# Moving the layer norms of batches 2 and 3 ahead of their batch and sending batch 1's through TensorE, in a fused attention and mixture-of-experts kernel

## The reference

```python
x = x + tanh(g_xattn[0]) * xattn(layernorm(x), ctx, ctx, wq, wk, wv, wo)
n = layernorm(x)                                  # 4 batches, 512 x 256 each
shared = sum over 2 experts of gelu(n @ up_s.T) @ down_s.T
probs  = softmax(n @ router_w.T)                  # 16 experts
gate   = probs where they are among the 4 highest of the token, else 0
routed = sum over 16 experts of (gelu(n @ up_r.T) * gate) @ down_r.T
out = x + tanh(g_ffn[0]) * (shared + routed)
```

## Time and profile before

| what | value |
|---|---|
| median of 3 runs | 535.67 us (534.5 to 536.22) |
| time of the profiled execution | 533.67 us |
| its span, first to last instruction | 531.9 us |
| around the span | 1.8 us |
| TensorE busy | 507.0 us, 95% of the span |
| VectorE, ScalarE, GpSimd busy | 67%, 58%, 52% |
| granted TensorE clock, mean | 0.997 |

### The profile page before, as it was taken

One profiled execution on the slowest core, in us unless ns is written; L12 is line 12 of the kernel. 1 busy time (PEld: TensorE's weight loads), 2 busy tenths in 40 slices (PEclk: granted clock), 3 DMA queues, 4 the chain that ended last, 5 costly groups with the idle time before them and its releaser, 6 DMA issues.

```text
span 531.9 us, 12294 instructions
## 1 busy us (share of the span) xinstructions
PE 507.0 (95%) x4386; PEld 421.4 (79%) x4386; DVE 355.7 (67%) x1150; ACT 310.4 (58%) x858; POOL 275.9 (52%) x213
## 2 busy tenths in 40 slices
PE   9888998999999999999999998899998999899996
PEld 5677787889988998888889786667776878678884
DVE  6868867658675677668866847486647665675554
ACT  3467767566757566766766956554536453644442
POOL 4899988779887978897998325430100010000000
PEclk9999999999999999999999999999999999999999
DMA  7362224011121101220221075514621372048021
GB/s 250 98 174 66 71 55 150 8 36 38 21 96 38 36 11 28 57 55 22 57 73 38 3 228 177 112 22 127 251 40 17 101 282 41 12 103 284 1 32 47
DMA packets 52075, 44.65 MB, mean 84 GB/s; under 512 B 33520, under 2 KB 35824, under 8 KB 52016
## 3 DMA queue, kind: packets, MB, share of 16 engines
q1 hardware_dynamic: 52016, 43.88, 29.3%
HBM read 30.62 MB, written 2.23 MB: 62 GB/s over the span
## 4 chain that ended last, share of the span: by engine, by line
PE 60%; POOL 11%; DVE 10%; issue 7%; SPq 6%; ACT 4%; DMA 2%; DVEq 0%; POOLq 0%; ACTq 0%
PE ring L1010 42%; SPq L354 5%; PE psO L1189 5%; PE psS L1010 4%; PE psS L1158 4%; PE psT L1170 4%; POOL arena L462 3%; POOL arena L464 2%; POOL prob L468 2%; DVE prob L819 2%; POOL wl L476 1%; DVE arena L768 1%; DMA pT<-pT 1%; POOL arena L455 1%; ACT oTh L563 1%
## 5 line engine op out<-in xcount | busy, mean ns | idle before, releaser
L1010 PE MATMUL ring<-xTh,wh 128*128 128x512 f32 x272 | 109.9, 404 | 1.8 <-DVE wl L840 1.4
L1010 PE MATMUL ring<-xTh,wl 128*128 128x512 f32 x272 | 106.8, 393 | 0.0
L1010 PE MATMUL ring<-xTl,wh 128*128 128x512 f32 x272 | 106.7, 392 | 0.0
L827 DVE TENSOR_TENSOR oTl<-prob,oTh 128x512 fp32r<-128x512 f32 x64 | 46.2, 722 | 58.7 <-ACT oTh L563 58.4
L468 POOL TENSOR_TENSOR prob<-prob,rinv 128x512 f32<-128x512 f32 x64 | 68.0, 1064 | 15.4 <-DVE rinv L921 15.4
L563 ACT ACTIVATE oTh<-prob 128x512 fp32r<-128x512 f32 x64 | 40.4, 631 | 60.9 <-DVE prob L819 36.1
L1010 PEld LDWEIGHTS ring<-xTh,wh 128*128 128x128 f32 x272 | 51.1, 188 | 14.9 <-issue 3.0
L637 ACT ACTIVATE pT<-psT 128x512 f32<-128x512 f32 x64 | 38.0, 593 | 40.3 <-PE psT L1170 40.3
L1010 PEld LDWEIGHTS ring<-xTh,wl 128*128 128x128 f32 x272 | 51.0, 188 | 11.3
L1010 PEld LDWEIGHTS ring<-xTl,wh 128*128 128x128 f32 x272 | 51.2, 188 | 10.9 <-issue 0.2
L547 ACT ACTIVATE sneg<-ring 128x512 f32<-128x512 f32 x72 | 42.5, 591 | 23.3 <-PE ring L1010 23.2
(11 more groups left out here) (123 smaller groups left out, 1230.3 us busy)
## 6 DMA issues: line engine op xcount, KB each, us to landing
arena<-gate_scratch SPq DMA_DIRECT2D x64, 256.0 KB, 6.3
raw<-in_e SPq DMA_DIRECT2D x18, 256.0 KB, 2.8
raw<-in_w SPq DMA_DIRECT2D x16, 256.0 KB, 3.8
arena<-arena SPq DMA_DIRECT2D x16, 256.0 KB, 3.1
pT<-pT SPq DMA_DIRECT2D x112, 32.0 KB, 2.0
arena<-arena SPq DMA_DIRECT2D x16, 192.0 KB, 3.5
out<-x SPq DMA_DIRECT2D x16, 128.0 KB, 6.2
x<-in_x SPq DMA_DIRECT2D x3, 512.0 KB, 3.8
```

The lines of the kernel that those rows point to most:

```text
L827: dve.tensor_tensor(lo, src, hi.bitcast(F32), ALU.subtract).then_inc(f_lo, 1)
L1010: last = pe.matmul(out, a, b, start=start and i == 0 and j == 0, stop=stop and i == n - 1 and j == 2, skip_group_check=check)
```

## The change

Three things change in the table of jobs and in the waits that guard them.

1. Norm 5 (batch 1) no longer goes through `turn`, `xhi` and `xlo`. Its statistics move from after step 3 to after step 4, its two halves of normalising from after step 4 to after steps 6 and 7, and after step 9 it takes the path of `xT`: 8 transposes on TensorE into the PSUM banks `psT` and `psO`, two copies by ScalarE, two subtractions by VectorE. The router follows after step 10 in place of 11, and `rexp`, `pick_a` and `pick_b` each one step sooner; `gT` stays after step 15.
2. Norms 6 and 7 (batches 2 and 3) are made earlier: the statistics after step -2 of the batch before (that is 5 steps sooner), the halves after steps -1 and 0, the `turn` after step 2 in place of 5. `xhi`, `xlo` and everything down to `gT` stand one step sooner.
3. Waits follow: `turn` waits for `z` of the batch before, batch 0's `back` no longer waits for `xlo` but for the end of the attention, and `r` waits for norm 5's `xTl`, since both use `psT`.

```diff
-        for b in range(B - 1):
-            for e, kind in ((3, "stat"), (4, "norm_a"), (4, "norm_b")):
+        for e, kind, n in ((4, "stat", B + 1), (6, "norm_a", B + 1), (7, "norm_b", B + 1), (9, "xT", B + 1),
+                           (10, "r", 1), (11, "rexp", 1), (12, "pick_a", 1), (13, "pick_b", 1), (15, "gT", 1)):
+            after[e].append((kind, n))
+        for b in range(1, B - 1):
+            for e, kind in ((-2, "stat"), (-1, "norm_a"), (0, "norm_b")):
                 after[b * NE + e].append((kind, B + b + 1))
-            for e, kind in ((5, "turn"), (9, "xhi"), (10, "xlo"), (11, "r"), (12, "rexp"), (13, "pick_a"),
-                            (14, "pick_b"), (15, "gT")):
+            for e, kind in ((2, "turn"), (8, "xhi"), (9, "xlo"), (10, "r"), (11, "rexp"), (12, "pick_a"),
+                            (13, "pick_b"), (14, "gT")):
                 after[b * NE + e].append((kind, b + 1))
...
                 elif kind == "turn":
-                    sp.wait_ge(xn_turned, n)
+                    sp.wait_ge(xn_turned, n - 1)
...
-                    act.wait_ge(xn_moved, 256 * n)
-                    if n == 1:
-                        act.wait_ge(down_pe, KC * NS)
-                    else:
-                        act.wait_ge(up_pe, NE * (n - 1))
-                        act.wait_ge(r_pe, n - 1)
+                    act.wait_ge(xn_moved, 256 * (n - 1))
+                    act.wait_ge(up_pe, NE * (n - 1))
+                    act.wait_ge(r_pe, n - 1)
...
-                act.wait_ge(xT_pe, min(j, B + 1))
-                if j > B + 1:
-                    act.wait_ge(xn_turned, j - B - 1)
+                act.wait_ge(xT_pe, min(j, B + 2))
+                if j > B + 2:
+                    act.wait_ge(xn_turned, j - B - 2)
...
-                    if n == 1:
-                        dve.wait_ge(oT_pe, CHUNKS // 2)
-                    else:
-                        dve.wait_ge(z_out, 4 * (n - 1))
+                    dve.wait_ge(z_out, 4 * (n - 1))
...
                     dve.wait_ge(y_out, GROUPS * (n + 1))
-                    if n + 1 < B:
+                    if n == 0:
+                        dve.wait_ge(oT_pe, CHUNKS // 2)
+                    elif n + 1 < B:
                         dve.wait_ge(xT_lo, B + n + 2)
...
+                elif job[0] == "xT" and job[1]:
+                    pe.wait_ge(p_out, CHUNKS)
+                    pe.wait_ge(oT_lo, CHUNKS // 2)
                 elif job[0] == "r":
-                    pe.wait_ge(p_out, CHUNKS)
+                    pe.wait_ge(xT_lo, B + 2)
                     pe.wait_ge(r_sub, job[1])
```

## The result

The changed kernel takes 523.1 us (median of 5 runs, 522.66 to 523.18) against 535.67 us (median of 5, 534.0 to 536.22): a ratio of 0.9774, 95% interval 0.9755 to 0.9793. The direction, the place and the mechanism were right; two sizes were not: what a stall costs, and how far the profile of the kernel before stood from its median. A later set of runs gave 522.84 against 535.31, ratio 0.9765 (0.9751 to 0.9778).

What follows compares the result with a forecast made beforehand. TensorE, busy 507.0 of 531.9 us, was taken as the bound, with 10.3 us of waits in the expert part. 5.4 + 4.3 = 9.7 us off gave 524.0 by the profile, 526.0 by the median; range 523.8 to 529.

Steps and rivals of the forecast that it cites:

- Part 2, the moves: Norms 6 and 7: moves done before `xhi`, all stalls of batches 1 and 2 go; 4.5 us, 4.3 counted.
- It sums to 10.3 us: TensorE's waits in the expert part, as listed: 7.2 + 2.2 + 0.9, nearly all on `rest_gated`.
- Part 1, norm 5: Batch 0: 5.49 us of stalls and 1.3 of low clock, less 0.9 for transposes; 5.4 us taken.
- it goes if the stall goes: Batch 0, after the 2.31 us stall: the low clock cost 1.3 us and vanishes with that stall.
- may stay: Batch 0's last stall, 0.47 us, may remain: table loads and `pick_a` share steps with weight rounding; 0.5 left for residues.
- L618 waits for nothing: Sign of being right: ScalarE's normalising no longer waits for GpSimd's `shift`; that wait was 3.14 us in batch 0.
- the rival named by the Trainium skill's rule: TensorE's clock falls once after the new transposes, which don't count as busy like matmuls: 1.3 us, 527.3; 5%.
- The shown median of 535.67 stands 2.0 above it, so by the median 526.0: From profiled run to median: 533.67 less 9.7 is 524.0, plus the same 2.0 gives 526.0.
- Late moves: Batches 1 and 2: moves still late, half of the two large stalls stays, perhaps a clock drop: 529; 9%.
- Router path: Batch 0 keeps its stalls, as ScalarE waits for transposes instead of moves: 528, or 529 with low clock; 9%.
- Gates held up: Small moves delay the gates' DMAs in batches 1 and 2, so every `gated` waits: 536 or more; 3%.
- No effect: VectorE's and ScalarE's work alone bounds the steps, so stalls only move: 535; 3%.

Runs made afterwards that it cites:

- part 2's: The kernel before with norms 6 and 7 made early and norm 5 left as before: 529.3 us, ratio 0.989.

## Why the prediction was right in kind and too small in size

**What bounds it, and where.** Right. All that was won lies at the places named in the earlier trace rows, and batch 3 is unchanged (0.96 and 0.97 us lost).

**Part 2, the moves.** Right in mechanism: `xhi` waits for no DMA, batches 1 and 2 lose nothing, and the traffic of the gates delayed nothing that counts: the 16 issues took 11.4 and 12.1 us beside it, not 10.5, and `xhi` still found its blocks there. The term "4.5 us; I keep 0.2 for small ones" was mis-sized: 4.3 forecast, 2.74 + 3.18 = 5.9 measured. The step that failed is the sum over the waits' view, "It sums to 10.3 us". A printed stall leaves out some 0.27 us at its two edges, and the router's 0.16 us at one. Four stalls and two waits of the router in batches 1 and 2 make 1.4 us, and the 0.2 kept for small ones was not needed; that is the difference of 1.6. The numbers to see it were there: the matmul durations of 0.50 in the earlier trace rows beside the usual 0.40.

**Part 1, norm 5.** 5.4 us forecast, 5.86 - 0.79 = 5.1 measured, but by errors that cancelled. The transposes cost 0.79 (0.9 forecast) and the router did not wait, as worked out. The stalls of 0.36 and 1.46 went. The edges of three fewer stalls gave 0.7 us more. Against that, 1.5 us of printed stalls stayed where 0.5 was allowed for. The 1.3 us of low clock are in the 8.57 and did go, but the step "it goes if the stall goes" counted as a cost of its own what was worth 0.2: without the low clock the router would have waited 0.7 us longer and the next stall been 0.3 longer, and the batch would have lost 8.36. That the sum came within 0.3 us was luck. The reason given for the stalls that "may stay", table loads and `pick_a` beside the weight rounding, was wrong: with the weight rest on VectorE they all go (two losses of 0.2 us, too short to be printed, are left), and table loads and rounding are still there. The sign "L618 waits for nothing" held for norm 5 alone; norms 6 and 7, whose `stat` and `norm_a` still stand one step apart, waited 2.3 and 1.7 us, at no cost to TensorE.

**The clock.** It did stay at 1.00 with the transposes in place, so the rival named by the Trainium skill's rule ("TensorE: Matmul & The Clock Gate", part 4) did not come about here. Two stretches of the changed kernel, the first with the eight transposes of step 9 (335.40) in it:

```profile
330.00:336.00 6.00, 6.00 (x30) 4.89 (x30) 4.09 (x6) 5.01 (x10) 3.35 (x3) 1.00 0.27 85
336.00:342.00 6.00, 6.00 (x30) 4.59 (x28) 4.39 (x8) 3.40 (x7) 2.62 (x2) 1.00 0.31 84
```

**From the profile to the median.** The second step that failed, and the larger error. "The shown median of 535.67 stands 2.0 above it, so by the median 526.0" carried the 2.0 us over to the changed kernel, as if it were a constant of the chip. It belonged to the kernel before: a longer stall in batch 2 and more low clock than in the one profiled run (1.0 to 1.6 us in three other profiles), and a later start of the expert part, by 0.3 to 0.9 us. The changed kernel has no such stall, and its profiled run (523.18) and its median (523.1) agree. Its start came at 307.10 and 306.71 in its two profiles; why its runs hold together within 0.55 us all the same isn't shown. Of the 2.9 us by which the gain was larger than forecast, 1.3 lie in the expert part (11.0 where 9.7 were summed) and 1.6 in this step. The account of the 12.6 us: 11.0 in the expert part, less 0.5 for the later start in this one profile, plus 2.0 by which the median of before stood above its profile, plus 0.1.

**The rivals.** Late moves: no. Router path: in part, 1.5 us of stalls, by a cause that wasn't named. (Its price was also added up wrongly: the stalls named, 1.36, and half of 2.31, less 0.5, do make 2.0 us, but "1.2 + 0.9 less the 0.5" makes 1.6.) Gates held up: no `gated` waits for a DMA. No effect: no.

## What to carry to other kernels

Price a stall of a matmul stream from start to start, not by the idle time that the view prints: here 0.27 us more for each, and losses of up to 0.3 us that aren't printed at all. If the kernel's runs spread more than the profile's waits explain, ask whether the spread comes from the stalls themselves, and take a second profile of the kernel before; a change that removes them can remove the distance between the profile and the median too. And before more work is moved off a busy engine, look at what its instructions last beside their undisturbed length: four subtractions given back to VectorE made it faster.

## What was not expected of the hardware

- The clock of TensorE fell behind six of nine gaps of 2.3 to 2.7 us, counted over six profiles of kernels with the old path in batch 0, and not behind the other three (2.29 us in part 2's, with a clock of 1.00 right after; 2.31 and 2.49 us in two others). It fell behind none of the gaps of 1.7 to 2.2 us. The low stretches held 7 to 13 matmuls.
- A low clock can cost next to nothing: 8.57 and 8.35 us lost in batch 0 with it, 8.36 and 8.39 without, because the next waits ended at the same time.
- One DMA issue of 16 alike can take 0.96 to 1.60 us where the others take 0.61, at the same place in the queue in all four profiles of before, and TensorE's stall behind it grows by the same amount.
- VectorE's 128x512 instructions of 0.68 us took 1.78, and its 128x1024 one 2.32 instead of 1.22, where GpSimd had begun a subtraction 0.1 to 0.6 us before; both lose 1.1 us. Where less of GpSimd's subtraction was left (begun 0.9 to 1.3 us before), the 128x512 ones took 0.9 to 1.0.
